# Dense attention, two score products before two maximum products instead of alternating: one reordering of TensorE's queue

## The reference

```python
# x: (4, 1024, 128) after the layernorm; 16 heads of size 8
q, k, v = split(x @ qkv_w + qkv_b)          # rotary applied to q and k
scores = einsum('bhqd,bhkd->bhqk', q, k) * 8 ** -0.5
attn   = softmax(scores, axis=-1)           # dense: 1024 x 1024 for each head
out    = einsum('bhqk,bhkd->bhqd', attn, v) @ out_w + out_b
```

## Time and profile before

| | us |
|---|---|
| median of 3 runs | 4111.85 |
| lowest, highest | 4109.42, 4115.35 |
| the profiled execution | 4106.34 |
| its span on the core | 4104.5 |
| 240 steps with maximum products, first to last product | about 382 to 1050 of the span |
| busy over the whole span: PE, DVE, ACT, POOL | 3445.3, 2658.6, 2592.4, 1415.0 |

### The profile page before, as it was taken

One profiled execution on the slowest core, in us unless ns is written; L12 is line 12 of the kernel. 1 busy time (PEld: TensorE's weight loads), 2 busy tenths in 40 slices (PEclk: granted clock), 3 DMA queues, 4 the chain that ended last, 5 costly groups with the idle time before them and its releaser, 6 DMA issues. The chain is left out here.

```text
span 4104.5 us, 54268 instructions
## 1 busy us (share of the span) xinstructions
PE 3445.3 (84%) x20368; PEld 1523.6 (37%) x20432; DVE 2658.6 (65%) x4320; ACT 2592.4 (63%) x4291; POOL 1415.0 (34%) x1418
## 2 busy tenths in 40 slices
PE   7989899999888888898887997799778597576776
PEld 4664222222212222222222665466554264232333
DVE  5336899999566666656665776577665123368887
ACT  2213777788789999899995885388543222225554
POOL 0520771100111010100003994399500514207886
PEclk9999999999999999999998999899989799797877
DMA  4131221111200110101000111011020121290001
GB/s 134 41 71 52 55 41 29 26 24 17 49 16 16 20 27 1 31 16 16 1 1 20 34 37 32 18 34 37 19 87 6 35 62 41 36 108 6 1 16 26
DMA packets 139708, 137.39 MB, mean 33 GB/s; under 512 B 41865, under 2 KB 104373, under 8 KB 139445
## 3 DMA queue, kind: packets, MB, share of 16 engines
q1 hardware_dynamic: 130676, 116.47, 13.4%
q0 software_dynamic: 8192, 16.79, 1.8%
q10 hardware_dynamic: 576, 0.66, 0.1%
HBM read 64.90 MB, written 33.82 MB: 24 GB/s over the span
## 5 line engine op out<-in xcount | busy, mean ns | idle before, releaser
L518 PE MATMUL PS<-t 50*128 50x512 bf16 (+2 forms) x3072 | 731.2, 394 | 171.5 <-ACT t L690 57.0
L841 DVE TENSOR_TENSOR t<-t 128x1536 f32<-128x1536 f32 (+1 forms) x384 | 587.5, 1596 | 104.2 <-ACT t L688 53.2
L748 DVE TENSOR_REDUCE t<-PS 128x1 f32<-128x1024 f32 x512 | 602.8, 1218 | 54.2 <-PE PS L510 46.8
L668 ACT ACTIVATE t<-PS 128x512 f32<-128x512 f32 x1024 | 529.8, 605 | 130.9 <-PE PS L518 121.1
L607 PE MATMUL PS<-t 128*9 128x512 f32 x4096 | 547.0, 606 | 19.9 <-DVE t L841 17.5
L518 PEld LDWEIGHTS PS<-t 50*128 50x128 bf16 (+2 forms) x3072 | 156.9, 94 | 956.1 <-ACT t L688 274.2
L690 ACT ACTIVATE t<-PS 128x1536 f32<-128x1536 f32 (+1 forms) x384 | 477.8, 1310 | 50.7 <-PE PS L518 30.0
L688 ACT ACTIVATE t<-PS 128x1536 f32<-128x1536 f32 (+1 forms) x384 | 476.6, 1311 | 40.4 <-PE PS L518 25.4
L1995 POOL TENSOR_TENSOR t<-t 128x512 f32<-128x512 f32 x128 | 160.0, 1270 | 572.0 <-ACT t L1860 570.6
L510 PE MATMUL PS<-t 48*128 48x512 bf16 x1024 | 339.8, 388 | 11.9 <-DMA t<-scr 6.0
L581 PE MATMUL PS<-t 128*128 128x384 f32 x532 | 261.9, 576 | 0.0
(11 more groups left out here) (403 smaller groups left out, 6516.8 us busy)
## 6 DMA issues: line engine op xcount, KB each, us to landing
t<-scr SPq DMA_DIRECT2D x384, 64.0 KB
t<-t SPq DMA_DIRECT2D x128, 128.0 KB, 2.3
scr<-t SPq DMA_DIRECT2D x96, 128.0 KB, 1.8
t<-t SPq DMA_DIRECT2D x16, 512.0 KB, 13.0
scr<-t SPq DMA_DIRECT2D x2, 2560.0 KB
t<-scr SPq DMA_DIRECT2D x16, 320.0 KB, 3.7
scr<-t SPq DMA_DIRECT2D x16, 320.0 KB, 2.6
t<-t SPq DMA_DIRECT2D x68, 32.0 KB, 2.0
```

Source lines behind the costliest of these rows:

```text
L518: return e.op.matmul(PS[:, bk, :], Kx[p // 4 % 2][lo:lo + rows, j, kb * 128:kb * 128 + 128], Qx[p // 4 % 2][lo:lo + rows, j, hf * 512:hf * ...
L668: e.op.activation(P[x % 4][:, 2 * hf + side, :], PS[:, bank((what, p, k, side, hf)), :], ACT.Exp, scale=S8).then_inc(*PW.up((p, k, side, hf)))
L748: e.op.tensor_reduce(MX[p % 2][:, side, qc:qc + 1], PS[:, b0:b0 + 2, :].rearrange("p a n -> p (a n)"), AX, ALU.max).then_inc(*DV.up(("max" ...
L841: e.op.tensor_tensor(o, o, SGM[(12 * p + 3 * blk + ti) % 3][:, 0:nu, :], ALU.mult).then_inc(*DG.up((p, blk, ti)))
```

## The change

In the branch `"step"`, the two score products of a side now stand together and the two maximum products of the other side behind them.

```diff
                                 for hf in range(2):
                                     bs = take(e, ring.next(), (what, p, k, side, hf), (PW, (p, k, side, hf)))
                                     score(bs, p, k, side, hf).then_inc(*SC.up((p, k, side, hf)))
-                                    if mate(p) is not None:
+                                if mate(p) is not None:
+                                    for hf in range(2):
                                         maxima(mate(p), k, 1 - side, hf)
```

## The result

| | before | changed |
|---|---|---|
| median of 4 runs, us | 4113.6 | 4152.4 |
| lowest, highest | 4109.42, 4115.56 | 4149.38, 4156.72 |
| profiled execution: span, us | 4104.5 | 4148.0 |

The ratio of the changed kernel to the one before is estimated at 1.0098, with a 95% interval from 1.0084 to 1.0113 (the two medians alone give 1.0094, 38.8 us). The forecast was 4157, 1.1% slower; it started from the median of the first three runs, 4111.85.

What follows compares the result with a forecast made beforehand. The bound was taken to be a 2.44 us loop through TensorE and ScalarE's first exp, no engine being full. 44.7 us from 208 steps plus 0.6 made 45.3; on the median 4111.85 that gave 4157 us, range 4147 to 4169.

Steps and rivals of the forecast that it cites:

- The loop: Ordinary step: first score product, its exp, last score product, weighted sums; said to close the whole step at 2.44 us.
- The front: First half of a step, second score product put ahead of the first maximum product: claimed to cost nothing now.
- The back: End of a step, last two maximum products behind the last score product's wait: step grows 0.21 to 0.22 us.
- 208 steps that I had called regular: Steps of the 240 with the ordinary shape: 0.215 us more each, 44.7 us together.
- The 240 steps: Stretch with maximum products, 668 us long: claimed to grow by 45.3 us, bounds 43.7 and 52.8.
- The seven odd steps: Steps among the 215 without the ordinary shape: four add nothing, three add 0.2 us each, 0.6 us together.
- The 19 steps with S3 late: Steps whose third score product is held up by a bank: claimed to add nothing, or 4.2 us if sides can't pass.
- The six steps with VectorE late: Steps whose third maximum product waits for VectorE: moving the last score product ahead was claimed to cost nothing.
- Strict order in the array: Rival, 8 in 100: no product passes a waiting one, even of the other side; time 4161 to 4165 us.
- Open weight loads: Rival, 5 in 100: a same-side product's weight load isn't hidden, so the loop grows by 0.31 us; time 4179 us.
- No slower: Rival, 8 in 100: last two maximum products run while the score product ahead still waits; step stays 2.44 us, time 4112.

Runs made afterwards that it cites:

- The swap of the waits: ScalarE's first exp of a step waits for the score product before the weighted sums: ratio to before 0.9979 on the kernel before, 1.0084 on the changed kernel.
- the front half alone: Kernel before with only the step's second score product moved ahead of its first maximum product: ratio 1.0005 to before.
- The back half alone: Kernel before with only the step's last score product moved ahead of its third maximum product: ratio 1.0097 to before.
- both tries: Kernel before with the weighted sums of the previous step moved directly ahead of the last score product (ratio 1.0292) or between the two sides (1.0046).
- the partners of the same side: Changed kernel with each step's maximum products taken from the same side as the score products in front of them: ratio 1.0287 to before.

## Why the prediction was right

**The loop.** S1, its exp, S4, what stands behind S4, the sums: as predicted. The swap of the waits shortened the step by just what it took from the loop, before and after the change.

**The front costs nothing.** Right, by the front half alone. M1 starts 0.01 us after S1 in the changed kernel, past S2.

**The back costs 0.21 to 0.22 us.** Right: 2.65 us, and the sums 0.54 us behind S4. The back half alone carries everything. Of the 208 steps that I had called regular, 204 grew by 44.1 us in all, 0.216 each, against the 0.215 that I had taken. Three more grew by 0.13, 0.16 and 1.5 us; the last is pair 0, step 2, which the changed kernel ran in part at half clock (granted 0.50 from 388 to 392 us). No term of my sum had the clock in it. The 208th is told next.

**The 240 steps grow by 45.3 us.** It was 41.3, below the 43.7 that I had given as the lower bound. The difference is mostly one place that I had counted as regular, pair 4, step 3, and the step behind it. Before, TensorE waited there for GpSimd:

```profile
489.78 0.27 PE L558 MATMUL PS<-t 128*32 128x128 f32 x1 [3.01 <-POOL t L923]
```

In the changed kernel, 6 us later by then, there is no such wait:

```profile
491.99 1.05 PE L608 MATMUL PS<-t 128*9 128x512 f32 x8
492.96 0.28 PE L558 MATMUL PS<-t 128*32 128x128 f32 x1
```

The two steps became 2.9 and 0.9 us shorter. Here a wait for another engine absorbed added time; I had not looked for one in the middle of the stretch. The seven odd steps, of which the second of the two is one, were to add 0.6 us and became 1.2 us shorter together.

**The 19 steps with S3 late cost nothing.** Their sum is 0.5 us, but not for my reason alone. Eleven of them paid 0.09 to 0.17 us: M3 no longer goes with S3 but only when S4's semaphore is met, up to 0.16 us later, and M4 another 0.23 behind. Five paid 0.02 to 0.05; in three of these (step 0 of the pairs 2, 10 and 18) the sums did come 0.22 us later behind S3, but S3 itself came 0.17 to 0.19 us sooner after S1. Three became shorter, by 1.1 us together, where waits for other work absorbed the time. I had asked only whether M3 can pass S4 in the array, not when S4's semaphore lets it. In pair 21, step 6, the passing is seen:

```profile
902.46 0.39 PE L518 MATMUL PS<-t 50*128 50x512 bf16 x1 [0.51 <-DVE t L825]
902.48 0.39 PE L510 MATMUL PS<-t 48*128 48x512 bf16 x1
902.69 0.38 PE L518 MATMUL PS<-t 50*128 50x512 bf16 x1
902.71 0.38 PE L510 MATMUL PS<-t 48*128 48x512 bf16 x1
```

M3 (902.48) stands behind S4 in the queue and started 0.21 us ahead of it (902.69). The six steps with VectorE late became shorter by 1.0 us together.

**The rivals.** Strict order in the array is refuted by the row above and by M1. Open weight loads would have shown 0.31 us behind S4 for M4; it is 0.23. "No slower" is refuted: in none of the 240 steps did M3 start before the end of the exp that S4 waited for; the nearest was 0.06 us behind it.

**The whole.** On the median the change was 38.8 us against 43.5 in the profiled pair; the runs of the changed kernel alone lie 7 us apart. So the mechanism and the 0.22 us a step were right, and the sum was 6.5 us too high on the medians. It came as near as it did in part because errors of both signs met: the half clock and the late M3 added about 1.5 us each, and waits took more than that away.

## What to carry to other kernels

Find the loop that closes a step first, and ask of a reordering only what it puts between the last wait of that loop and its end. The same pair of products is free ahead of the wait and costs a place of the array behind it. Before moving a long block into a gap, follow who needs the products on both its sides: in both tries here a block in the gap of one loop became a part of another.

## What the runs showed of the hardware

Matmuls on different partitions of the array do not start in the order of the queue, once their semaphores are met. In the run with the partners of the same side, three score products are out within 0.60 us, of which the last takes 0.38: two of them ran at once. S1 and S2 are of one side and start 0.22 us apart, so it is S3, the first of the other side, that ran beside S1, and it stands behind S2, M1 and M2 in the queue. In 162 of the 240 steps it starts 0.01 us after S1. In the changed kernel M1 starts 0.01 us after S1 in 232 of 240 steps, past S2. The Trainium skill, TensorE: Matmul & The Clock Gate, Part 3 (The mechanism), has matmuls strictly in program order; these traces disagree, by up to three products of the queue. A product whose semaphore is not met does hold everything behind it: M3 never started before S4's exp had ended, in 240 steps.

The order in which an instruction's two semaphores are named in the code is worth 0.06 us: with the product's wait named first, ScalarE's first exp of an ordinary step starts 0.42 us after S1 instead of 0.48. In the traces with the swap no step has 0.48; before, 138 of the 240 had it. Why the order matters is not shown.
